# First expert layer: one product of 512 columns for both parts of x in every second block

## The chip, the cores and the metric
One core of a Trainium2 chip runs the kernel. The metric is the device time of one execution in microseconds, and it is given as the median of several runs. All data are float32; the large products run in the float32r form.

## The reference, cut to what matters
```python
x = x + gnn(layernorm(x), adj, Wq, Wk, Wv)      # 4096 rows of 256
xf = layernorm(x)
# the router picks 2 of E = 8 experts for each row
for e in range(8):
    h = relu(xf @ W1[e] + b1[e])                # W1[e]: 256 x 1024
    y = h @ W2[e] + b2[e]                       # W2[e]: 1024 x 256
    out = out + combine[:, e:e+1] * y
x = x + out
```
The kernel computes each expert for only those rows that chose it.

## The kernel before, in words
The first 440 us are attention and routing; the change leaves them alone. Then the experts run. The rows of an expert lie together in memory, and they are worked off in tiles of T = 256 rows (TS = 2 groups of 128). Here there are 37 tiles: 32 full ones and 5 half ones. Experts with an odd number of groups end with a half tile, for which TensorE streams 128 columns instead of 256, while the other engines still handle 256.

Each float32 operand is split in two float32r parts, a "hi" (the rounded value) and a "lo" (the rest). A product is then hi*hi + hi*lo + lo*hi. For a tile n the work is:

- **rows_turned** (L1372 to L1379): TensorE transposes the tile's rows into `psX`. ScalarE rounds them into `x_hi` (L1593, `part_of_x`), VectorE takes the rest into `x_lo` (L1076, `rest_of_x`). It is done for tile n+1 near the end of tile n, and the next tile's first product waits for `x_lo` (semaphore `xl_ready`, L1384).
- **first(hc)** (L1387 to L1394), eight times, for blocks of 128 hidden units: six products into one of four PSUM buffers `psH[:, hc % 4]`, of which columns 0 to 255 are used. It waits until the buffer's last block has been read (`hf_ready`, L1388).
- ScalarE (`tile_of`, L1603 to L1608) then applies bias and relu twice from the same PSUM buffer: to `h_f` in float32 (a piece of `z_all`, L1607) and to `h_hi` in float32r (L1608, signals `hf_ready`).
- VectorE (`tile`, L1111 to L1124) subtracts: `h_lo = h_f - h_hi` (L1122, signals `hl_ready`).
- **second(hc)** (L1396 to L1406): for each group of 128 rows a product of `h_hi` with both parts of the second weights side by side (512 columns, L1402) and one of `h_lo` with the large part (256 columns, L1404), into `psE`. It waits for `hl_ready` (L1397), and in block 0 for the previous tile's `psE` to be read, too (L1399).

TensorE's order is written out by hand with LAG = 3: first(0), first(1), first(2), first(3), second(0), first(4), second(1), ... first(7), second(4), rows_turned(n+1), second(5), second(6), second(7). All engines run their instructions in the order in which they are written.

VectorE has more to do in a tile. At the middle (hc == 4) it scales and adds the previous tile's result (`add_rows`, L1098, waits for rows gathered by GpSimd) and computes the gate (`gate_of`, L1084 to L1090). In an expert's first and second tile ("splitting tiles", 14 of 37) it also splits one piece of the next expert's weights in each odd block: `w_hi` (L1104) before the block's `h_lo`, `w_lo` (L1109) behind it. At the tile's end come `x_lo` (L1076), the copy of the row marks (L1079) and the sums of `psE` (L1133, L1136).

`wait_alone` (L344) is a wait as an instruction of its own, so that the value may come from a register.

Of the kernel before, what the change touches and what calls it, by code (L numbers as in the profile page):

```python
# [23 lines left out]
F32 = mybir.dt.float32  # L24
F32R = mybir.dt.float32r
# [8 lines left out]
ALU = mybir.AluOpType  # L34
ACT = mybir.ActivationFunctionType
AX = mybir.AxisListType

P = 128
# [7 lines left out]
CC = C // P  # L46
HC = H // P
# [12 lines left out]
T = 256  # L60
# [12 lines left out]
def attention_and_experts(nc, x, adj, Wq, Wk, Wv, Wr, W1, b1, W2, b2, out):  # L73
    ctx = ExitStack()

    def sb(name, shape, dt, stack=ctx):
        return stack.enter_context(nc.sbuf_tensor(name, shape, dt))
# [4 lines left out]
    def sem(name):  # L82
        return ctx.enter_context(nc.semaphore(name))

    with ctx:
# [149 lines left out]
        ffn = ExitStack()  # L235
# [3 lines left out]
        w1_lo = sb("w1_lo", [P, 2, CC, H], F32R, ffn)  # L239
        w2_parts = sb("w2_parts", [P, 2, HC, 2, C], F32R, ffn)  # L240
        x_in = sb("x_in", [P, TS, CX], F32, ffn)
        x_hi = sb("x_hi", [P, CC, T], F32R, ffn)
        x_lo = sb("x_lo", [P, CC, T], F32R, ffn)

        h_f = z_all[:].rearrange("p t c -> p (t c)")[:, 0:HC * T].rearrange("p (k t) -> p k t", t=T)
        b2_rows = z_all[:].rearrange("p t c -> p (t c)")[:, HC * T:HC * T + E * C].rearrange("p (e c) -> p e c", c=C)
# [85 lines left out]
        b2_loaded = sem("b2_loaded"); x_ps = sem("x_ps");  # L332
        w_raw = [sem("w1_raw_loaded"), sem("w2_raw_loaded")]; w_hi = sem("w_hi"); w_split = sem("w_split");
        xin_loaded = sem("xin_loaded"); xh_ready = sem("xh_ready"); xl_ready = sem("xl_ready")
        h_ps = sem("h_ps"); hf_ready = sem("hf_ready"); hl_ready = sem("hl_ready")
        e_ps = sem("e_ps"); yo_ready = sem("yo_ready"); yp_ready = sem("yp_ready")
        marks_ready = sem("marks_ready"); tok_taken = sem("tok_taken"); less_ready = sem("less_ready"); gate_step = sem("gate_step")
        acc_ready = sem("acc_ready"); acc_clear = sem("acc_clear"); y_ready = sem("y_ready"); y_scattered = sem("y_scattered"); y_free = sem("y_free"); tok_kept = sem("tok_kept")
# [5 lines left out]
        def wait_alone(eng, what, value):  # L344

            eng.wait_ge(what, value)
            if not isinstance(value, int):
                eng.sem_inc(passed[eng.engine], 1)
# [252 lines left out]
        def _(dve):  # L601
# [471 lines left out]

            def rest_of_x(n):
                dve.wait_ge(xh_ready, n + 1)
                dve.tensor_tensor(x_lo[:].rearrange("p k t -> p (k t)"), psX[:], x_hi[:].bitcast(F32).rearrange("p k t -> p (k t)"),  # L1076
                                  ALU.subtract).then_inc(xl_ready, 1)
                wait_alone(dve, tok_taken, n + 1)
                dve.tensor_copy(marks[:], x_in[:, :, TOK:TOK + 2].bitcast(U32)).then_inc(marks_ready, 1)  # L1079
# [21 lines left out]
            def next_weights_hi(e, c):  # L1101
                raw, hi, lo = weight_part(c, (e + 1) % 2)
                wait_alone(dve, w_raw[c // (SPLITS // 2)], e * 16 + 32)
                dve.tensor_copy(hi, raw).then_inc(w_hi, 1)  # L1104
# [6 lines left out]
            def tile(n, e, split=None, first=False, alone=None):  # L1111
                for hc in range(HC):
                    if hc == HC // 2:
                        if not first:
                            add_rows(n)
                        gate_of(n, e)
                    splitting = split is not None and hc % 2 == 1
                    c = (split or 0) * (SPLITS // 2) + hc // 2
                    if splitting:
                        next_weights_hi(e, c)  # L1120
                    dve.wait_ge(hf_ready, n * HC + hc + 1 + 4)
                    dve.tensor_tensor(h_lo[:, hc, :], h_f[:, hc, :], h_hi[:, hc, :].bitcast(F32), ALU.subtract).then_inc(hl_ready, 1)  # L1122
                    if splitting:
                        next_weights_lo(e, c)  # L1124
                if alone is not None:
                    with dve.If(alone):
                        for c in range(SPLITS // 2, SPLITS):
                            next_weights_hi(e, c)
                            next_weights_lo(e, c)
                rest_of_x(n + 1)  # L1130
                for q in range(TS):
                    dve.wait_ge(e_ps, n * TS + q + 1)
                    dve.tensor_tensor(y_part[:, q, :], psE[:, q, C:2 * C], row(b2_rows, e), ALU.add).then_inc(yp_ready, 1)  # L1133
                for q in range(TS):
                    wait_alone(dve, yp_ready, n * TS + q + 1)
                    dve.tensor_tensor(y_sum[:, q, :], psE[:, q, 0:C], y_part[:, q, :], ALU.add).then_inc(yo_ready, 1)  # L1136
# [23 lines left out]
        def _(pe):  # L1160
# [221 lines left out]
            def tile(n, b, parts):  # L1382

                wait_alone(pe, xl_ready, n + 1)  # L1384
                cols = slice(0, parts * P)

                def first(hc):  # L1387
                    wait_alone(pe, hf_ready, n * HC + hc + 1)  # L1388
                    m = slice(hc * P, (hc + 1) * P)
                    for k in range(CC):  # L1390
                        pe.matmul(psH[:, hc % 4, cols], w1_hi[:, b, k, m], x_hi[:, k, cols], start=(k == 0), stop=False)  # L1391
                        pe.matmul(psH[:, hc % 4, cols], w1_hi[:, b, k, m], x_lo[:, k, cols], start=False, stop=False)  # L1392
                        last = pe.matmul(psH[:, hc % 4, cols], w1_lo[:, b, k, m], x_hi[:, k, cols], start=False, stop=(k == CC - 1))  # L1393
                    last.then_inc(h_ps, 1)  # L1394

                def second(hc):  # L1396
                    wait_alone(pe, hl_ready, n * HC + hc + 1 + HC)  # L1397
                    if hc == 0:
                        wait_alone(pe, yo_ready, n * TS + TS)  # L1399
                    for q in range(parts):  # L1400
                        m = slice(q * P, (q + 1) * P)
                        pe.matmul(psE[:, q, :], h_hi[:, hc, m], w2_parts[:, b, hc].rearrange("p s c -> p (s c)"),  # L1402
                                  start=(hc == 0), stop=False)
                        last = pe.matmul(psE[:, q, 0:C], h_lo[:, hc, m], w2_parts[:, b, hc, 0, :], start=False, stop=(hc == HC - 1))  # L1404
                        if hc == HC - 1:
                            last.then_inc(e_ps, 1 if q + 1 < parts else TS - q)  # L1406
                for hc in range(HC + LAG):
                    if hc < HC:
                        first(hc)
                    if hc == HC:  # L1410
                        rows_turned(n + 1)
                    if hc >= LAG:
                        second(hc - LAG)
# [16 lines left out]
        def _(act):  # L1430
# [159 lines left out]

            def part_of_x(n):
                act.wait_ge(x_ps, n + 1 + 1)
                act.copy(x_hi[:].rearrange("p k t -> p (k t)"), psX[:]).then_inc(xh_ready, 1)  # L1593
                act.activation(less_exp[:], x_in[:, :, LESS], ACT.Exp).then_inc(less_ready, 1)
            part_of_x(0)

# [6 lines left out]
            def tile_of(n, e):  # L1603
                for hc in range(HC):
                    wait_alone(act, hl_ready, n * HC + hc + 1)
                    act.wait_ge(h_ps, n * HC + hc + 1)
                    act.activation(h_f[:, hc, :], psH[:, hc % 4, 0:T], ACT.Relu, bias=b1T[:, e * HC + hc:e * HC + hc + 1])  # L1607
                    act.activation(h_hi[:, hc, :], psH[:, hc % 4, 0:T], ACT.Relu, bias=b1T[:, e * HC + hc:e * HC + hc + 1]).then_inc(hf_ready, 1)  # L1608
                part_of_x(n + 1)
# [30 lines left out]
```

## Time and profile before

| | us |
|---|---|
| median of 3 runs (896.09 to 896.87) | 896.53 |
| the profiled execution, its own time | 893.15 |
| its span, first to last instruction | 891.4 |
| TensorE busy in it | 704.7 |
| VectorE busy | 574.5 |
| ScalarE busy | 455.6 |
| GpSimd busy | 428.0 |

The profile is one execution. A timeline row has the start of an instruction in us from the span's start, its duration in us, the engine (PE is TensorE's products, DVE VectorE, ACT ScalarE), the line, what it writes and reads, and, in brackets, how long the engine was idle before it and what ended that. Instructions of one engine overlap: the next one can start before the last one's end, so the distance between two starts (the pitch) is what an instruction costs in a dense stream, and its duration is what a waiting engine sees.

### The profile page before, as it was taken

How to read it: one execution, taken by the hardware profiler on the slowest of the kernel's cores; microseconds unless marked ns; L12 is line 12 of the kernel's file. 1: busy time of each engine (PE TensorE's matmuls, PEld its weight loads, DVE VectorE, ACT ScalarE, POOL GpSimd, SP SyncE). 2: the span in 40 equal slices, each digit the busy share in tenths (PEclk: the TensorE clock that was granted, in tenths of full speed). 3: DMA queues.
4: the chain of work that ended last, by engine and by line, in shares of the span. 5: the costliest groups of instructions: out<-in, count | busy, mean ns of one | idle time of the engine just before them, and what ended most of it. 6: DMA issues, size and time to landing. Idle time of an engine off the chain costs nothing.

```text
span 891.4 us, 22902 instructions
## 1 busy us (share of the span) xinstructions
PE 704.7 (79%) x6398; PEld 640.0 (72%) x6399; DVE 574.5 (64%) x2054; ACT 455.6 (51%) x1286; POOL 428.0 (48%) x482
## 2 busy tenths in 40 slices
PE   2559999999876724261299999999999999999994
PEld 1448888888763614260299888888988899898993
DVE  8745666666639697426185766767666685776554
ACT  2535665655561403242255666555556555656663
POOL 2177777777730187773224334333433344444433
PEclk8569999999997555565599999999999999999997
DMA  9875334551101222447623242233314242112121
GB/s 292 266 193 134 103 85 125 137 132 34 46 17 48 68 81 94 139 160 247 194 94 101 56 157 66 90 118 107 112 57 154 70 151 85 44 61 76 43 65 39
DMA packets 89586, 96.72 MB, mean 109 GB/s; under 512 B 10427, under 2 KB 78533, under 8 KB 89404
## 3 DMA queue, kind: packets, MB, share of 16 engines
q1 hardware_dynamic: 70860, 61.46, 23.5%
q0 software_dynamic: 18672, 34.66, 12.2%
q8 instruction: 20, 0.33, 0.2%
q14 instruction: 34, 0.28, 0.1%
HBM read 82.25 MB, written 30.33 MB: 126 GB/s over the span
## 4 chain that ended last, share of the span: by engine, by line
PE 32%; issue 7%; DMA 6%; DVE 3%; POOL 2%; SPq 1%; DVEq 1%; ACT 1%; POOLq 0%; ACTq 0%
PE psE L1402 10%; PE psH L1391 5%; PE psH L1393 5%; PE psH L1392 5%; PE psE L1404 5%; DMA acc<-out,tok_next 4%; POOL out L576 2%; PE psX L1378 2%; SPq L423 1%; DMA expert_in<-pad_row 1%; DVE y_out L1098 1%; DVE h_lo L1122 1%; DMA out<-y_out,tok_now 1%; SPq L424 0%; DVE w_parts L1109 0%
## 5 line engine op out<-in xcount | busy, mean ns | idle before, releaser
L1607 ACT ACTIVATE z_all<-psH,b1T 128x256 f32<-128x256 f32 x296 | 142.6, 482 | 160.3 <-PE psH L1393 159.7
L1402 PE MATMUL psE<-w_parts,h_hi 128*128 128x512 f32 x552 | 209.6, 406 | 3.4 <-DVE h_lo L1122 2.7
L493 POOL DMA_INDIRECT nbr<-xn_rows,idx x160 | 164.6, 1029 | 83.8 <-issue 81.6
L1122 DVE TENSOR_TENSOR h_lo<-z_all,h_hi 128x256 fp32r<-128x256 f32 x296 | 122.5, 424 | 81.3 <-ACT h_hi L1608 81.2
L1391 PE MATMUL psH<-x_hi,w_hi 128*128 128x256 f32 (+1 forms) x592 | 166.2, 281 | 10.7 <-issue 6.1
L1393 PE MATMUL psH<-x_hi,w_lo 128*128 128x256 f32 (+1 forms) x592 | 165.9, 280 | 0.0
L1392 PE MATMUL psH<-x_lo,w_hi 128*128 128x256 f32 (+1 forms) x592 | 165.6, 280 | 0.0
L1404 PE MATMUL psE<-w_parts,h_lo 128*128 128x256 f32 x552 | 154.9, 281 | 0.0
L1608 ACT ACTIVATE h_hi<-psH,b1T 128x256 fp32r<-128x256 f32 x296 | 142.1, 480 | 0.0
L576 POOL DMA_INDIRECT out<-y_out,tok_now x74 | 77.5, 1047 | 112.9 <-DVE y_out L1098 93.4
L1391 PEld LDWEIGHTS psH<-x_hi,w_hi 128*128 128x128 f32 x592 | 112.3, 190 | 21.8 <-issue 14.1
L1402 PEld LDWEIGHTS psE<-w_parts,h_hi 128*128 128x128 f32 x552 | 103.8, 188 | 20.9 <-issue 5.5
L1393 PEld LDWEIGHTS psH<-x_hi,w_lo 128*128 128x128 f32 x592 | 112.4, 190 | 0.0
L1392 PEld LDWEIGHTS psH<-x_lo,w_hi 128*128 128x128 f32 x592 | 112.4, 190 | 0.0
L1404 PEld LDWEIGHTS psE<-w_parts,h_lo 128*128 128x128 f32 x552 | 104.3, 189 | 0.0
L567 POOL DMA_INDIRECT acc<-out,tok_next x74 | 77.3, 1044 | 47.8 <-POOL tok_next L562 33.5
L690 DVE CUSTOM_DVE_ANT_0 prod<-q_sb,nbr 128x256 f32<-128x256 f32 x160 | 58.2, 423 | 60.2 <-DMA nbr<-xn_rows,idx 34.5
L521 POOL DMA_INDIRECT expert_in<-late,pos x64 | 67.6, 1056 | 37.5 <-issue 19.3
L1219 PEld LDWEIGHTS psY<-diag,nbr 128*128 128x128 f32 x640 | 80.0, 198 | 6.8 <-ACT diag L1471 5.1
L1219 PE MATMUL psY<-diag,nbr 128*128 128x128 f32 x640 | 80.3, 282 | 5.0 <-ACT diag L1471 5.0
L572 POOL COPY tok_now<-tok_next 128x2 uint32<-128x2 uint32 x37 | 8.2, 221 | 102.4 <-DMA acc<-out,tok_next 102.4
L1208 PE MATMUL psQ<-wqk,xT 128*128 128x256 f32 x128 | 38.1, 422 | 17.7 <-ACT xT L1482 17.7
(335 smaller groups left out, 1173.7 us busy)
## 6 DMA issues: line engine op xcount, KB each, us to landing
w_raw<-in_L_ffn_W SPq DMA_DIRECT2D x16, 1024.0 KB, 5.5
x_in<-expert_in SPq DMA_DIRECT2D x38, 260.0 KB, 3.1
adj_even<-in_adj SPq DMA_DIRECT2D x4, 2048.0 KB, 13.0
late<-in_adj SPq DMA_DIRECT2D x4, 2048.0 KB
x_all<-in_x SPq DMA_DIRECT2D x4, 1024.0 KB, 9.1
xn_rows<-z_all SPq DMA_DIRECT2D x4, 1024.0 KB
out<-x_all SPq DMA_DIRECT2D x4, 1024.0 KB, 4.6
expert_in<-pad_row SPq DMA_DIRECT2D x8, 390.0 KB, 8.4
```

The costliest lines, as they stand in the source:

```text
L493: pool.indirect_dma_start(nbr[:, u * K + k, :], None, xn_rows, bass.IndirectOffsetOnAxis(ap=idx[:, u, k:k + 1], axis=0), bounds_check=ROW0 ...
L567: pool.indirect_dma_start(acc[:, q, :], None, out, bass.IndirectOffsetOnAxis(ap=tok_next[:, q:q + 1], axis=0), bounds_check=N - 1, oob_is_ ...
L576: pool.indirect_dma_start(out, bass.IndirectOffsetOnAxis(ap=tok_now[:, q:q + 1], axis=0), y_out[:, q, :], None, bounds_check=N - 1, oob_is ...
L1122: dve.tensor_tensor(h_lo[:, hc, :], h_f[:, hc, :], h_hi[:, hc, :].bitcast(F32), ALU.subtract).then_inc(hl_ready, 1)
L1219: last = pe.matmul(psY[:, c * P:(c + 1) * P], nbr[:, u * K + k, c * P:(c + 1) * P], diag[:, u % 2 * K + k, :], start=(k == 0), stop=(k == ...
L1391: pe.matmul(psH[:, hc % 4, cols], w1_hi[:, b, k, m], x_hi[:, k, cols], start=(k == 0), stop=False)
L1392: pe.matmul(psH[:, hc % 4, cols], w1_hi[:, b, k, m], x_lo[:, k, cols], start=False, stop=False)
L1393: last = pe.matmul(psH[:, hc % 4, cols], w1_lo[:, b, k, m], x_hi[:, k, cols], start=False, stop=(k == CC - 1))
L1402: pe.matmul(psE[:, q, :], h_hi[:, hc, m], w2_parts[:, b, hc].rearrange("p s c -> p (s c)"), start=(hc == 0), stop=False)
L1404: last = pe.matmul(psE[:, q, 0:C], h_lo[:, hc, m], w2_parts[:, b, hc, 0, :], start=False, stop=(hc == HC - 1))
L1607: act.activation(h_f[:, hc, :], psH[:, hc % 4, 0:T], ACT.Relu, bias=b1T[:, e * HC + hc:e * HC + hc + 1])
L1608: act.activation(h_hi[:, hc, :], psH[:, hc % 4, 0:T], ACT.Relu, bias=b1T[:, e * HC + hc:e * HC + hc + 1]).then_inc(hf_ready, 1)
```

## The change
In odd blocks (hc = 1, 3, 5, 7) TensorE multiplies the large weights with `x_hi` and `x_lo` side by side: one product of 512 columns takes the place of two of 256 columns, for each k. Columns 0 to 255 of the PSUM buffer then hold the `x_hi` half (to which the `w1_lo` product is still added), columns 256 to 511 the `x_lo` half. ScalarE adds the bias to the second half and writes `h_f`; VectorE adds the first half to it; ScalarE applies relu to the sum and writes `h_hi`; VectorE applies relu to `h_f` and subtracts `h_hi` in one instruction. On VectorE the addition for block hc + 1 stands ahead of the `h_lo` of block hc. Even blocks are computed as before. In half tiles the merged product has 2 x 128 columns.

```diff
-        x_hi = sb("x_hi", [P, CC, T], F32R, ffn)
-        x_lo = sb("x_lo", [P, CC, T], F32R, ffn)
+        x_parts = sb("x_parts", [P, CC, 2, T], F32R, ffn)
+        x_hi, x_lo = x_parts[:, :, 0, :], x_parts[:, :, 1, :]
...
@@ VectorE, rest_of_x(n)
-                dve.tensor_tensor(x_lo[:].rearrange("p k t -> p (k t)"), psX[:], x_hi[:].bitcast(F32).rearrange("p k t -> p (k t)"),
+                dve.tensor_tensor(x_lo, psX[:].rearrange("p (k t) -> p k t", k=CC), x_hi.bitcast(F32),
                                   ALU.subtract).then_inc(xl_ready, 1)
...
@@ VectorE, tile(...)
                     if splitting:
                         next_weights_hi(e, c)
+                    if hc % 2 == 0:
+                        wait_alone(dve, ht_ready, n * (HC // 2) + hc // 2 + 1)
+                        dve.tensor_tensor(h_f[:, hc + 1, :], psH[:, (hc + 1) % 4, 0:T], h_f[:, hc + 1, :], ALU.add).then_inc(hs_ready, 1)
                     dve.wait_ge(hf_ready, n * HC + hc + 1 + 4)
-                    dve.tensor_tensor(h_lo[:, hc, :], h_f[:, hc, :], h_hi[:, hc, :].bitcast(F32), ALU.subtract).then_inc(hl_ready, 1)
+                    if hc % 2 == 0:
+                        dve.tensor_tensor(h_lo[:, hc, :], h_f[:, hc, :], h_hi[:, hc, :].bitcast(F32), ALU.subtract).then_inc(hl_ready, 1)
+                    else:
+                        dve.scalar_tensor_tensor(h_lo[:, hc, :], h_f[:, hc, :], 0.0, h_hi[:, hc, :].bitcast(F32), ALU.max, ALU.subtract).then_inc(hl_ready, 1)
                     if splitting:
                         next_weights_lo(e, c)
...
@@ TensorE, first(hc)
                     for k in range(CC):
-                        pe.matmul(psH[:, hc % 4, cols], w1_hi[:, b, k, m], x_hi[:, k, cols], start=(k == 0), stop=False)
-                        pe.matmul(psH[:, hc % 4, cols], w1_hi[:, b, k, m], x_lo[:, k, cols], start=False, stop=False)
+                        if hc % 2:
+                            pe.matmul(psH[:, hc % 4].rearrange("p (s t) -> p s t", s=2)[:, :, cols], w1_hi[:, b, k, m],
+                                      x_parts[:, k, :, cols], start=(k == 0), stop=False)
+                        else:
+                            pe.matmul(psH[:, hc % 4, cols], w1_hi[:, b, k, m], x_hi[:, k, cols], start=(k == 0), stop=False)
+                            pe.matmul(psH[:, hc % 4, cols], w1_hi[:, b, k, m], x_lo[:, k, cols], start=False, stop=False)
                         last = pe.matmul(psH[:, hc % 4, cols], w1_lo[:, b, k, m], x_hi[:, k, cols], start=False, stop=(k == CC - 1))
...
@@ ScalarE, tile_of(n, e)
                     wait_alone(act, hl_ready, n * HC + hc + 1)
+                    if hc % 2:
+                        wait_alone(act, hl_ready, n * HC + hc + 1)
+                        act.wait_ge(h_ps, n * HC + hc + 1)
+                        act.activation(h_f[:, hc, :], psH[:, hc % 4, T:2 * T], ACT.Identity, bias=b1T[:, e * HC + hc:e * HC + hc + 1]).then_inc(ht_ready, 1)
+                        act.wait_ge(hs_ready, n * (HC // 2) + hc // 2 + 1)
+                        act.activation(h_hi[:, hc, :], h_f[:, hc, :], ACT.Relu).then_inc(hf_ready, 1)
+                        continue
```
The cast into `x_hi` (L1593) gets the same reshaping as `x_lo`, and `hs_ready` and `ht_ready` are new semaphores.

## Rows read from the trace of the kernel before

**Rows 1.** The page: busy time of TensorE, and its granted clock over the span
```profile
PE 704.7 (79%) x6398; PEld 640.0 (72%) x6399; DVE 574.5 (64%) x2054; ACT 455.6 (51%) x1286; POOL 428.0 (48%) x482
...
PEclk8569999999997555565599999999999999999997
```

**Rows 2.** Waits of TensorE, 438 to 880 us: us in total, times, longest
```profile
PE psE L1402 <- DVE h_lo L1122: 2.7, 5, 1.0
```

**Rows 3.** Five tiles by window: busy PE, PEld, DVE, ACT, POOL; clock, DMA share, GB/s
```profile
619.65:631.69 12.04, 11.94 (x86) 10.99 (x85) 10.10 (x29) 7.09 (x18) 5.40 (x7) 1.00 0.44 153
607.90:619.65 11.75, 11.74 (x84) 11.05 (x85) 9.50 (x27) 7.08 (x18) 2.80 (x4) 1.00 0.14 46
857.96:869.64 11.68, 11.68 (x86) 10.96 (x85) 6.93 (x21) 7.08 (x18) 4.45 (x7) 1.00 0.23 67
489.52:499.62 10.10, 8.94 (x70) 8.17 (x69) 7.48 (x23) 7.08 (x18) 3.27 (x6) 1.00 0.24 70
869.64:878.59 8.95, 8.95 (x70) 8.15 (x68) 6.33 (x19) 7.09 (x18) 2.59 (x5) 1.00 0.22 67
```

**Rows 4.** Timeline: the start of a full tile without weight splitting, three engines
```profile
846.27 0.28 PE L1391 MATMUL psH<-x_hi,w_hi 128*128 128x256 f32 x1
...
847.54 0.47 ACT L1608 ACTIVATE h_hi<-psH,b1T 128x256 fp32r<-128x256 f32 x1
847.55 0.28 PE L1393 MATMUL psH<-x_hi,w_lo 128*128 128x256 f32 x1
...
847.90 0.48 ACT L1607 ACTIVATE z_all<-psH,b1T 128x256 f32<-128x256 f32 x1
...
848.04 0.43 DVE L1122 TENSOR_TENSOR h_lo<-z_all,h_hi 128x256 fp32r<-128x256 f32 x1 [0.49 <-ACT h_hi L1608]
...
849.07 0.40 PE L1402 MATMUL psE<-w_parts,h_hi 128*128 128x512 f32 x1
...
849.30 0.28 PE L1404 MATMUL psE<-w_parts,h_lo 128*128 128x256 f32 x1
```

**Rows 5.** Timeline: products of a half tile
```profile
489.80 0.27 PE L1391 MATMUL psH<-x_hi,w_hi 128*128 128x128 f32 x1
...
491.47 0.27 PE L1391 MATMUL psH<-x_hi,w_hi 128*128 128x128 f32 x1
```

**Rows 6.** Timeline: one tile's first h_lo and the product that waited for it
```profile
513.61 0.43 DVE L1122 TENSOR_TENSOR h_lo<-z_all,h_hi 128x256 fp32r<-128x256 f32 x1 [0.97 <-ACT h_hi L1608]
...
514.43 0.47 PE L1402 MATMUL psE<-w_parts,h_hi 128*128 128x512 f32 x1
```

**Rows 7.** Page and groups by line: nearest prices for the new instructions
```profile
L1136 DVE TENSOR_TENSOR y_sum<-psE,y_part 128x256 f32<-128x256 f32 x74 | 27.6, 415 | 0.2 <-DVE y_part L1133 0.2
L1444 ACT ACTIVATE z_all<-x_all,less_mean,rstd 128x256 f32<-128x256 f32 x24 | 12.1, 585 | 0.0
L1458 ACT COPY xt<-z_all 128x256 f32<-128x256 f32 x7 | 2.8, 403 | 0.0
```

**Rows 8.** Timeline: the end of the tile before the one in rows 4
```profile
843.21 0.47 ACT L1607 ACTIVATE z_all<-psH,b1T 128x256 f32<-128x256 f32 x1 [0.58 <-PE psH L1393]
...
844.35 0.59 ACT L1593 CAST x_hi<-psX 128x512 fp32r<-128x512 f32 x1 [0.30 <-PE psX L1378]
...
844.97 0.69 DVE L1076 TENSOR_TENSOR x_lo<-psX,x_hi 128x512 fp32r<-128x512 f32 x1 [0.43 <-ACT x_hi L1593]
```

**Rows 9.** Timeline of VectorE in the splitting tile 619.65 to 631.69
```profile
621.92 0.43 DVE L1122 TENSOR_TENSOR h_lo<-z_all,h_hi 128x256 fp32r<-128x256 f32 x1 [0.98 <-ACT h_hi L1608]
...
623.54 0.42 DVE L1122 TENSOR_TENSOR h_lo<-z_all,h_hi 128x256 fp32r<-128x256 f32 x1
...
625.72 0.88 DVE L1098 SCALAR_TENSOR_TENSOR y_out<-y_sum,gate,acc 128x256 f32<-128x256 f32 x2 [0.49 <-issue]
...
627.39 0.43 DVE L1122 TENSOR_TENSOR h_lo<-z_all,h_hi 128x256 fp32r<-128x256 f32 x1
...
630.62 0.68 DVE L1076 TENSOR_TENSOR x_lo<-psX,x_hi 128x512 fp32r<-128x512 f32 x1
```

More of the change, by code:

```diff
@@ L334, in attention_and_experts @@
         xin_loaded = sem("xin_loaded"); xh_ready = sem("xh_ready"); xl_ready = sem("xl_ready")
-        h_ps = sem("h_ps"); hf_ready = sem("hf_ready"); hl_ready = sem("hl_ready")
+        h_ps = sem("h_ps"); hf_ready = sem("hf_ready"); hs_ready = sem("hs_ready"); ht_ready = sem("ht_ready"); hl_ready = sem("hl_ready")
         e_ps = sem("e_ps"); yo_ready = sem("yo_ready"); yp_ready = sem("yp_ready")
@@ L1592, in part_of_x @@
                 act.wait_ge(x_ps, n + 1 + 1)
-                act.copy(x_hi[:].rearrange("p k t -> p (k t)"), psX[:]).then_inc(xh_ready, 1)
+                act.copy(x_hi, psX[:].rearrange("p (k t) -> p k t", k=CC)).then_inc(xh_ready, 1)
                 act.activation(less_exp[:], x_in[:, :, LESS], ACT.Exp).then_inc(less_ready, 1)
```

## The prediction
> **What bounds the kernel now.** I read the page first: TensorE is the busiest engine, and its clock is at its upper level, 2.4 GHz, through nearly all of the second half, where the change lies [rows 1]. Then the waits: over the whole expert stage TensorE waited 2.7 us for `h_lo`, in five places [rows 2]. Then the tiles one by one: in a full tile without weight splitting TensorE is busy for all of the 11.68 us [rows 3]. So the stage is a dense stream of TensorE, and everything ScalarE and VectorE do is hidden. The question is by how little. VectorE is busy 10.10 of 12.04 us in a splitting tile, and ScalarE 7.08 of 8.95 us in a half tile [rows 3]; both get more work here. The 37 tiles are 14 splitting, 18 full without splitting, 5 half.
>
> **TensorE: the merged product.** From 846.27 to 849.07 there are 24 products of 256 columns, 0.117 us each; the 512-column product has a pitch of 0.23 to the next [rows 4]. Two of 256 cost 0.234, so the merge buys between nothing and some 5 ns, the rounding of the row. I take 1 ns: 32 full tiles x 4 blocks x 2 = 256 pairs, 0.3 us. The Trainium skill (TensorE: Matmul & The Clock Gate, Back-to-back issue gap) gives about 131 ns per 512-column product as the sustained pace and would promise 256 x 0.10 = 26 us; the existing 512-column products show 0.23, and by that the page does not hold here.
>
> In a half tile 15 pitches take 1.67 us, 0.111 each for 128 columns [rows 5]: a merged product of 256 columns at 0.117 replaces two, 0.105 less. That is 8 per tile, 0.84 us, if TensorE still bounds there.
>
> **The longer chain at a tile's start.** Before: `h_hi` of block 0 starts at 847.54 and takes 0.47, `h_lo` starts at 848.04 and ends at 848.47. Where TensorE did wait for `h_lo`, its product came 514.43 - 514.04 = 0.39 us after the end (block 0 has two waits) [rows 6]. So second(0) could have started at 848.86; it started at 849.07, when the stream reached it [rows 4]. The slack is 0.21 us. Now VectorE must do the addition for block 1 ahead of that `h_lo`. ScalarE's first instruction of block 1 starts at 847.90, where L1607 did, and takes 0.48: 848.38. I add 0.15 for the signal and VectorE's separate wait (my choice: signals between engines show 0.03 to 0.04, as from 848.01, the end of `h_hi`, to 848.04 [rows 4], a separate wait some 0.1 more; bounds 0.04 and 0.25). The addition reads PSUM and SBUF like L1136, 0.415 us [rows 7]. A following `h_lo` starts some 0.34 later (four VectorE instructions in 1.62 us, one of them of 512 columns [rows 9]; its whole duration, 0.43, is the upper bound). So `h_lo` starts 848.53 + 0.34 = 848.87, ends 849.30, and second(0) starts 849.69: **0.61 us late**, in every full tile. Bounds 0.45 and 0.75.
>
> **The end of a tile.** ScalarE's last block starts at 843.21 [rows 8]. New: 0.48, 0.15, 0.42 for the addition, 0.04, then the relu, at 844.30. Its price isn't in the trace: a copy from SBUF to SBUF takes 0.403, an activation from SBUF with per-row bias and scale 0.585 [rows 7]. I take 0.40, as it reads neither bias nor scale, with a pitch of 0.31 (L1607 at 0.48 has about 0.36 to the next [rows 4], so overlap is 0.1). The Trainium skill (ScalarE: Activation LUTs) puts an ACTIVATE with immediate operands at 186 + 0.833 N ns, so 399 ns by an estimate from that page. The cast to `x_hi` then starts at 844.61 instead of 844.35, `x_lo` 0.26 later too. `x_lo` ended at 845.66, and with 0.39 the next tile could start at 846.05; it started at 846.27 [rows 4, 8]. Slack 0.22, so 0.05 us late. With the relu at 0.585 it is 0.2.
>
> Full tiles without splitting: 18 x (0.61 + 0.05) = 11.9 us. Inside such a tile the chain is covered: an odd block now takes 0.48 + 0.15 + 0.42 + 0.04 + 0.40 + 0.04 + 0.45, 2.0 us from PSUM to `h_lo`, while TensorE reaches its second() six segments of 0.70 later, 4.2 us.
>
> **Splitting tiles.** VectorE's pair of blocks (h_lo, w_hi, h_lo, w_lo) has a period of 623.54 - 621.92 = 1.62 us; the middle (y_out and gate) takes 627.39 - 625.72 = 1.67; `x_lo` starts at 630.62, and the next tile 0.39 after its end [rows 3, 9]. That is already a tight chain. The addition costs 0.34 a pair, the fused max and subtract 0.02 more: 1.98. VectorE starts 2.25 us into the tile (848.53 - 846.27) and doesn't pause: 2.25 + 4 x 1.98 + 1.67 + 0.68 + 0.39 = 12.9 us. Against 11.75 for an expert's first tile and 12.04 for its second that is +1.15 and +0.9 (its 0.49 us pause before y_out is filled): 7 x 2.05 = 14.4 us. I add 2.0 us (0.15 a tile) because second(4) and second(6), which need `h_lo` behind an addition, come within 0.2 us of VectorE's schedule. VectorE becomes the bound here.
>
> **Half tiles.** ScalarE's pair takes 0.37 + 0.36 for the even block, then 0.48 + 0.15 + 0.42 + 0.04 + 0.31: 2.13 us. TensorE needs 2 x 1.01 = 2.03 before and 1.82 after, so ScalarE bounds, standing still while VectorE adds. First activation at 0.87 (six products, result, signal), first relu at 2.69, fourth at 2.69 + 3 x 2.13 = 9.08. In the middle VectorE's 1.67 us stands between the `h_lo` of block 3 (ending its pitch at 5.6) and the addition of block 5, which so starts at 7.3 instead of 6.5: +0.8. The last relu starts at 9.85, `x_hi` 10.16 to 10.75, `x_lo` 10.79 to 11.48, next tile 11.87, against 10.10 [rows 3]: +1.75, four times. The kernel's last tile ends with second(7): relu until 10.25, `h_lo` 10.7, wait 0.2, products 0.5: 11.4 against 8.95: +2.45. Together 9.5 us. TensorE's 0.84 a tile is lost behind it.
>
> **Sum:** 11.9 + 14.4 + 2.0 + 9.5 - 0.3 = 37.5 us. The profiled execution took 893.15 (span 891.4 and 1.75 around it) and would take 930.6; the median lies 3.4 above the profiled time, so the median goes to 934.0. Three full tiles close an expert; their idle time for the change of expert may swallow the 0.05, no more. No DMA is added or moved; GpSimd is paced by `y_out` and slides with it.
>
> **Rivals.**
> - *A, the lag covers the chain* (faster). For it: three blocks of lead, and 2.0 us against 4.2 within a tile. Then only TensorE's own saving counts: 0.3 + 5 x 0.84 = 4.5, 892.0 us. It decides at the start of a tile: addition and its handover would have to cost under 0.21 us, and L1136 alone speaks against it. If moreover a merged product went at the pace of one of 256 columns, 256 x 0.117 = 30 us would go, 866; the 0.23 speaks against that. By the page's 131 ns it would be about 870. Chance 4% for all of it, 1% of it for the pace.
> - *B, only tiles' starts are hurt* (VectorE and ScalarE overlap better than in my chains; the 0.49 us pauses show room): 37 x 0.66 = 24.4, 921. 20%.
> - *C, the forecast*: 934. 55%.
> - *D, the handshake binds in every pair*: relu 0.585, a handover 0.25, VectorE slowed beside other traffic. 18 x 0.95, 7 x (1.9 + 1.4), 4 x 2.6 + 3.2: 54 us, 950. 18%.
> - *E, nothing measurable*: half-tile gain and stalls cancel; needs most of B to vanish. 3%.
>
> **How the numbers follow.** What can be told from no change is about 0.2%, 1.8 us. Faster is A, same E, slower B, C and D. The range: the low ends of my costs (0.45 x 18, splitting 12.7 us, half +1.0) give 22 to 24 us, B at a lower handover 18; the high ends are D's, up to 57. So 914 to 954.
>
> **What the profile after would show.** The 512-column product of the first layer with a pitch of 0.23. In a plain tile: waits of L1402 on `h_lo` of about 0.6 us once a tile, and a length of 12.35. In splitting tiles: 12.9 to 13.1, VectorE without idle time between the first addition and `x_lo`. In half tiles: ScalarE waiting for the addition 0.6 us in every pair, 11.9 us in all. TensorE's clock stays at 2.4 GHz, as its pauses stay short. I would be wrong if second(0) started on time, if the merged product's pitch were under 0.2, or if the splitting tiles kept to 12.

## The result and the profile after

The changed kernel takes 945.28 us (median of 3 runs, 944.59 to 947.32) against 896.53: a ratio of 1.055, 95% interval 1.052 to 1.058. It is 48.8 us slower. The forecast was 934.0, slower, with a range of 914 to 954. The sign held, and so did the mechanism in splitting and half tiles; in plain tiles (full, without splitting) a longer chain counts than the one that was forecast, and the size was some 11 us short. The profiled execution took 944.59 us, its span is 942.8.

The page of the changed kernel, busy time and granted clock, to be read beside [rows 1]:

```profile
span 942.8 us, 22921 instructions
PE 723.8 (77%) x6102; PEld 630.0 (67%) x6103; DVE 626.9 (66%) x2202; ACT 449.6 (48%) x1286; POOL 433.0 (46%) x482
...
PEclk8569999999976555555999999999999999999997
```

TensorE issues 296 products less. VectorE is busy 52 us more; the 148 additions of 0.425 us add up to 62.9, and where instructions overlap the busy time counts once. ScalarE is busy less than before: its relu of the odd blocks, which reads SBUF and adds no bias, takes 0.418 us, the one from PSUM with bias 0.467. No engine is short of time by these sums; the loss shows as waits. What TensorE waited for in the expert stage (440 to 932 us), and what ScalarE waited for:

```profile
PE psE L1412 <- DVE h_lo L1126: 27.2, 43, 1.2
...
PE psH L1401 <- issue: 11.6, 13, 1.8
PE psH L1401 <- DVE x_parts L1076: 8.0, 14, 1.7
```
```profile
ACT h_hi L1621 <- DVE z_all L1123: 116.6, 148, 1.9
```

TensorE's wait for `h_lo` was 2.7 us before [rows 2] and is 27.2 us, mostly once a tile. All three waits come to 46.8 us, for 13.4 before. TensorE's busy time grew, too, by 19.1 us to 723.8, with fewer products. Part of that is waiting too: the profile counts a product's whole duration (0.28 us) as busy, while the next one could start after 0.117, so a pause looks shorter than the delay that it makes (below, 0.43 us idle for 0.59 late). Part is a lower clock in three tiles (last section). ScalarE now stands 116.6 us for VectorE's additions, 0.60 us in a usual odd block and 0.79 in the mean of the 148.

Six tiles by window (as in [rows 3]: length, busy PE, PEld, DVE, ACT, POOL, clock, DMA share, GB/s): plain, an expert's second splitting tile, its first one, half, the tile behind that half tile, and the last half tile.

```profile
894.12:906.68 12.56, 12.12 (x76) 10.58 (x77) 8.41 (x25) 6.95 (x18) 4.51 (x6) 1.00 0.21 63
642.22:655.61 13.39, 12.41 (x77) 10.57 (x77) 11.50 (x34) 6.96 (x18) 6.36 (x7) 1.00 0.38 139
629.00:642.22 13.22, 12.30 (x76) 10.57 (x77) 10.48 (x30) 6.85 (x18) 2.64 (x4) 1.00 0.11 38
496.19:509.18 12.99, 8.91 (x60) 7.52 (x61) 8.89 (x27) 6.74 (x18) 5.07 (x7) 1.00 0.21 64
509.18:523.41 14.23, 13.75 (x77) 12.02 (x77) 10.69 (x31) 6.97 (x18) 3.19 (x5) 0.88 0.10 25
919.49:931.27 11.78, 8.87 (x60) 7.47 (x60) 7.70 (x23) 6.73 (x18) 4.21 (x6) 1.00 0.22 67
```

Every kind of tile got longer. Taken over the trace, from a tile's first product to the next tile's:

| kind of tile | before, mean us | after, mean us | together, us | forecast, us |
|---|---|---|---|---|
| 18 full without splitting | 12.12 | 13.02 | +16.2 | +11.9 |
| 14 splitting | 12.11 | 13.52 | +19.8 | +16.4 |
| 5 half | 10.05 | 12.88 | +14.2 | +9.5 |

Together that is +50.2 us. The expert stage also began 2.5 us later than in the profile of before (443.3 against 440.7 us) and its tail was 1.3 us shorter, which gives the 51.4 us between the two spans. The medians differ by less, 48.8, as the profiled execution of before was 3.4 us faster than its median and that of the changed kernel 0.7. The late start is no effect of the change: `merged_only`, below, starts its stage at 444.3 us and has a span of 892.1, and `before_lag4`, which has nothing of the change, starts it at 443.4.

The start of the plain tile whose counterpart is in [rows 4], in the changed kernel:

```profile
895.83 0.47 ACT L1619 ACTIVATE z_all<-psH,b1T 128x256 f32<-128x256 f32 x1
...
896.45 0.42 DVE L1123 TENSOR_TENSOR z_all<-psH,z_all 128x256 f32<-128x256 f32 x1 [1.21 <-ACT z_all L1619]
...
896.79 0.42 DVE L1126 TENSOR_TENSOR h_lo<-z_all,h_hi 128x256 fp32r<-128x256 f32 x1
...
896.91 0.42 ACT L1621 ACTIVATE h_hi<-z_all 128x256 fp32r<-128x256 f32 x1 [0.60 <-DVE z_all L1123]
...
897.60 0.47 PE L1412 MATMUL psE<-w_parts,h_hi 128*128 128x512 f32 x1 [0.43 <-DVE h_lo L1126]
```

The tile began at 894.12. ScalarE's bias instruction ends at 896.30, the addition starts 0.15 later, `h_lo` another 0.34 later and ends at 897.21, and the product comes 0.39 after that. 897.60 is 3.48 us into the tile, where the kernel before was at 2.80: 0.59 late by the pitch of the product ahead of it and 0.09 from a slower start. ScalarE's second wait for `hl_ready` in odd blocks, which stands in the diff, shows no price: L1619 starts 0.35 us behind L1625 (895.48), as L1607 started 0.36 behind L1608 before [rows 4].

### The profile page after: what moved, and what is told of

Same layout as the page of the kernel before. It is cut to its first block, busy times and chain, and to the rows that moved or that the text cites. A ratio compares the mean times of both kernels' runs of the same rounds, so it can differ in the third digit from the quotient of the medians.

```text
span 942.8 us, 22921 instructions
## 1 busy us (share of the span) xinstructions
PE 723.8 (77%) x6102; PEld 630.0 (67%) x6103; DVE 626.9 (66%) x2202; ACT 449.6 (48%) x1286; POOL 433.0 (46%) x482
## 4 chain that ended last, share of the span: by engine, by line
PE 24%; DVE 12%; issue 11%; ACT 5%; DMA 1%; SPq 1%; DVEq 1%; POOL 1%; ACTq 0%; POOLq 0%
PE psE L1412 8%; PE psE L1414 4%; PE psH L1403 3%; DVE h_lo L1126 3%; PE psH L1401 3%; PE psH L1398 3%; ACT z_all L1619 2%; PE psH L1402 2%; ACT h_hi L1625 2%; DVE x_parts L1076 1%; DVE z_all L1123 1%; DVE y_out L1098 1%; DVE w_lo L1109 1%; PE psX L1384 1%; DVE w_parts L1109 1%
## 5 line engine op out<-in xcount | busy, mean ns | idle before, releaser
L1412 PE MATMUL psE<-w_parts,h_hi 128*128 128x512 f32 x552 | 213.7, 411 | 27.6 <-DVE h_lo L1126 27.2
L1403 PE MATMUL psH<-x_parts,w_lo 128*128 128x256 f32 (+1 forms) x592 | 166.2, 281 | 0.0
L1123 DVE TENSOR_TENSOR z_all<-psH,z_all 128x256 f32<-128x256 f32 x148 | 62.9, 425 | 103.7 <-ACT z_all L1619 102.2
L1621 ACT ACTIVATE h_hi<-z_all 128x256 fp32r<-128x256 f32 x148 | 61.8, 418 | 116.6 <-DVE z_all L1123 116.6
L1403 PEld LDWEIGHTS psH<-x_parts,w_lo 128*128 128x128 f32 x592 | 115.0, 194 | 0.0
L1624 ACT ACTIVATE z_all<-psH,b1T 128x256 f32<-128x256 f32 x148 | 68.5, 463 | 93.6 <-PE psH L1403 93.4
L1398 PE MATMUL psH<-x_parts,w_hi 128*128 128x512 f32 (+1 forms) x296 | 108.7, 392 | 0.0
L1401 PE MATMUL psH<-x_parts,w_hi 128*128 128x256 f32 (+1 forms) x296 | 86.6, 293 | 19.8 <-issue 11.6
L1402 PE MATMUL psH<-x_parts,w_hi 128*128 128x256 f32 (+1 forms) x296 | 84.2, 285 | 0.0
L1401 PEld LDWEIGHTS psH<-x_parts,w_hi 128*128 128x128 f32 x296 | 57.3, 194 | 35.3 <-issue 30.4
L1619 ACT ACTIVATE z_all<-psH,b1T 128x256 f32<-128x256 f32 x148 | 70.3, 475 | 20.7 <-PE psH L1403 19.5
L1128 DVE SCALAR_TENSOR_TENSOR h_lo<-z_all,h_hi 128x256 fp32r<-128x256 f32 x148 | 62.9, 425 | 13.7 <-ACT h_hi L1621 11.6
```

The lines of the kernel that those rows point to most:

```text
L1123: dve.tensor_tensor(h_f[:, hc + 1, :], psH[:, (hc + 1) % 4, 0:T], h_f[:, hc + 1, :], ALU.add).then_inc(hs_ready, 1)
L1398: pe.matmul(psH[:, hc % 4].rearrange("p (s t) -> p s t", s=2)[:, :, cols], w1_hi[:, b, k, m], x_parts[:, k, :, cols], start=(k == 0), stop ...
L1619: act.activation(h_f[:, hc, :], psH[:, hc % 4, T:2 * T], ACT.Identity, bias=b1T[:, e * HC + hc:e * HC + hc + 1]).then_inc(ht_ready, 1)
```

## The experiments

Twelve kernels; each is compared with runs of the kernel before on the same chip. Tile lengths are from one profile each. The plain tile used is the last but two, which starts at 894.12 in the changed kernel and at 846.27 in the kernel before, or, in only_block_1 and only_block_5, the next one. It is the shortest of its neighbours in the changed kernel (12.74, 12.56, 12.81 us; before, all three took 11.69), so means over all tiles are given where they matter.

**1. merged_only.** Only TensorE's part of the change; the odd blocks' `x_lo` half is left out of the result.

```diff
-                    if hc % 2 == 0:
-                        wait_alone(dve, ht_ready, n * (HC // 2) + hc // 2 + 1)
-                        dve.tensor_tensor(h_f[:, hc + 1, :], psH[:, (hc + 1) % 4, 0:T], h_f[:, hc + 1, :], ALU.add).then_inc(hs_ready, 1)
...
-                    if hc % 2:
-                        wait_alone(act, hl_ready, n * HC + hc + 1)
...
```


> TensorE keeps the merged product in the odd blocks; ScalarE and VectorE are as in the kernel before and read only columns 0 to 255, so the x_lo half of the odd blocks is left out of the result. Theory H (the loss is the handshake between ScalarE and VectorE, the product costs what the two cost): 892 to 896 us; the merged product's pitch to the next is 0.23 us, plain full tiles 11.69 us, half tiles up to 0.8 us shorter. Rival P (the wide product or its operand layout is dear on TensorE): well over 905 us, with plain tiles over 12 us.

Measured: 895.49 us, 0.998 of before (0.997 to 0.999). The window of the plain tile and of a half tile:

```profile
847.06:858.72 11.66, 11.66 (x79) 10.60 (x77) 7.05 (x21) 7.08 (x18) 4.46 (x7) 1.00 0.23 67
813.96:823.67 9.71, 8.32 (x63) 7.42 (x61) 7.08 (x22) 6.95 (x18) 2.89 (x6) 1.00 0.25 72
```
The time and both kinds of tile lie where theory H had them. 11.66 for 11.68 in the plain tile: eight merged products save 0.02 us or so. That is all the change can bring there. In half tiles TensorE is busy 0.6 us less (8.32 for 8.95), but they are only 0.3 us shorter in the mean (9.73 for 10.05). The whole gain of the idea, with the addition for nothing, is 1.7 us, and by the interval between 0.5 and 3.

**2. split_products.** The changed kernel with the merge undone on TensorE alone.

```diff
-                            pe.matmul(psH[:, hc % 4].rearrange("p (s t) -> p s t", s=2)[:, :, cols], w1_hi[:, b, k, m],
-                                      x_parts[:, k, :, cols], start=(k == 0), stop=False)
+                            pe.matmul(psH[:, hc % 4, cols], w1_hi[:, b, k, m], x_hi[:, k, cols], start=(k == 0), stop=False)
+                            pe.matmul(psH[:, hc % 4, T:T + parts * P], w1_hi[:, b, k, m], x_lo[:, k, cols], start=False, stop=False)
```


> The changed kernel, but TensorE makes two products of 256 columns again in odd blocks, one into columns 0 to 255, one into 256 to 511; ScalarE and VectorE work as in the changed kernel. H: 944 to 947 us, as the changed kernel (945.3): TensorE's saving is 1 ns a pair in full tiles and hidden in half tiles. P: back towards 900 us.

Measured: 945.63 us, the changed kernel's time, as expected. With merged_only it splits the change in two: the loss is on ScalarE's and VectorE's side, and within 1 or 2 us the merge neither makes nor mends any of it.

**3. add_behind.** The three lines of VectorE's addition stand behind `h_lo` of block hc.

> The changed kernel, with VectorE's addition for block hc + 1 moved behind the h_lo of block hc instead of ahead of it. H: the wait of 0.6 us for h_lo at the start of each plain tile goes (18 tiles, 11 us), the splitting tiles gain about 0.3 us each as VectorE starts earlier (4 us), half tiles about 0.3 us: 926 to 933 us. Rival Q (it is only VectorE's added time, wherever it stands): 942 us or more.

Measured: 955.34 us (1.058 to 1.071 of before), 10 us slower than the changed kernel. The expectation failed on its sign. The product second(0) of a plain tile was on time, as expected, but another one was late, at the other end of the tile (timeline of the plain tile, a product of second(7); then the tile's window):

```profile
915.08 0.47 PE L1412 MATMUL psE<-w_parts,h_hi 128*128 128x512 f32 x1 [0.46 <-DVE h_lo L1125]
```
```profile
903.46:916.16 12.70, 12.10 (x77) 10.59 (x77) 8.57 (x25) 6.73 (x18) 4.71 (x7) 1.00 0.20 62
```
So the 0.6 us at the tile's start is not a loss that stands alone. ScalarE stood 2.04 us in the middle of the tile (1.10 in the changed kernel), because y_out, the gate and now also `h_lo` of block 4 stood ahead of the addition for block 5:

```profile
911.92 0.42 ACT L1621 ACTIVATE h_hi<-z_all 128x256 fp32r<-128x256 f32 x1 [2.04 <-DVE z_all L1128]
```
In the splitting tile that was read VectorE got a pause of 0.15 us in three of four pairs, since the relu was later than the `h_lo` that wants it. My new theory: each tile has one chain through ScalarE and VectorE from end to end, and TensorE's waits only show where the slack runs out first.

**4. all_full.** TensorE treats half tiles as full ones (`tile(before + full, b, TS)`).

> The changed kernel, with TensorE treating the five half tiles as full ones (twice the columns, same result). H: in half tiles ScalarE and VectorE set the pace (12.9 us), so TensorE's extra 2.7 us a tile cost nothing, the half tiles stay at 12.5 to 13 us, and the stretches of 3.4 us at 1.2 GHz behind three of them go, 0.9 us each: 940 to 944 us. If TensorE or its waits set the pace in half tiles: up to 5 x 2.7 = 13 us more, 958 us.

Measured: 944.15 us, where 940 to 944 was expected. The half tile and the tile behind it:

```profile
788.67:802.24 13.57, 12.13 (x77) 10.59 (x77) 9.17 (x27) 6.95 (x18) 5.60 (x7) 1.00 0.20 60
802.24:815.62 13.38, 12.37 (x77) 10.60 (x77) 10.63 (x31) 6.95 (x18) 2.98 (x6) 1.00 0.09 22
```
TensorE was busy 3.2 us longer in the half tile, and the tile only 0.2 us (13.35 in the changed kernel; the five in the mean 13.26 for 12.88, slightly over what was expected; of the 1.9 us that this makes for all five, 0.8 lie in the last one). ScalarE and VectorE set its pace. The tile behind it fell from 14.16 to 13.38 us, with the granted clock at 1.00 in place of 0.88.

**5. dve_load.** The kernel before plus VectorE's added time alone.

```diff
+                    if hc % 2 == 0:
+                        dve.tensor_tensor(spare[:, hc // 2, :], b2_rows[:, 0, :], b2_rows[:, 1, :], ALU.add)
```


> The kernel before, with one more VectorE addition of 256 columns (constants, into unused memory, nobody waits for it) ahead of the h_lo of each even block: VectorE's added time without the handshake. If VectorE's added time by itself makes the loss in splitting tiles: 14 tiles by 0.4 to 0.9 us, 902 to 910 us, plain tiles still 11.69 us. If the loss is that ScalarE and VectorE wait for each other (H): under 902 us, and the rest of the 49 us belongs to the waiting.

The added instruction takes 0.42 us, like the addition. Measured: 902.65 us, 1.007 of before (1.005 to 1.009), at the lower edge of what was expected if the load alone made the loss of the splitting tiles. The plain tile and a second splitting tile:

```profile
858.30:869.95 11.65, 11.65 (x86) 10.95 (x85) 8.15 (x25) 7.08 (x18) 4.88 (x7) 1.00 0.21 67
627.36:640.30 12.94, 12.37 (x85) 11.02 (x85) 11.47 (x34) 7.08 (x18) 6.13 (x7) 1.00 0.39 143
```
VectorE's load alone costs 6 us of the 49. Its profile, of an execution 2.8 us slower than the median, has them almost wholly in splitting tiles: 7.8 us over the 14, of the 19.8 that the change adds to them, with 0.9 in the half tiles and 0.4 in the 18 plain ones. So in splitting tiles the load alone explains a good third. If load and waiting simply add up, which was not tested, some 42 us are left to the waiting for each other.

**6. only_block_1 and 7. only_block_5.** The change in one odd block a tile (`if hc == 1`, `if hc == 5` in place of `if hc % 2`, and one count a tile for the two semaphores).

> The changed kernel with the merged product and the addition in block 1 alone; blocks 3, 5 and 7 as in the kernel before. H: a quarter of the additions, but all of the wait at a tile's start: plain tiles 12.3 us, together 912 to 920 us. If each merged block costs the same: 896.5 + 49 / 4 = 909 us.

> The same with block 5 alone, whose chain lies in the middle of a tile, behind VectorE's y_out and gate. H: no wait at the start; plain tiles 11.69 to 11.75 us, splitting tiles 0.1 to 0.4 us longer, half tiles up to 1 us: 899 to 906 us. If each merged block costs the same: 909 us.

Measured: 914.97 us (1.019 to 1.023) and 905.63 us (1.009 to 1.013). The plain tile with block 1, then with block 5:

```profile
878.91:891.29 12.38, 11.95 (x84) 10.96 (x83) 7.27 (x22) 7.14 (x18) 4.58 (x7) 1.00 0.22 63
```
```profile
868.25:879.93 11.68, 11.68 (x85) 10.89 (x84) 7.45 (x22) 7.02 (x18) 4.47 (x7) 1.00 0.22 68
```
Both times lie in the range of theory H, and not at the 909 of equal shares, though the second is only 3.4 us from it. The price of a merged block depends on where it stands: 18.6 us for block 1, 9 us for block 5, of which nothing in the plain tile shown (1.4 us over all 18) and half in the half tiles (11.04 us in the mean, for 10.05). Blocks 3 and 7 were not tried alone.

**8. behind_gate_late.** As add_behind, with the gate two blocks later.

```diff
-                    if hc == HC // 2:
-                        if not first:
-                            add_rows(n)
-                        gate_of(n, e)
+                    if hc == HC // 2 and not first:
+                        add_rows(n)
+                    if hc == HC // 2 + 2:
+                        gate_of(n, e)
```


> The addition behind h_lo as in add_behind (955.3), and VectorE's gate (0.86 us) moved from in front of block 4 to in front of block 6, so that only y_out stands ahead of the addition for block 5. Add_behind had its wait of 0.6 us moved from the start of a plain tile to its end, with ScalarE standing 2.0 us for the addition of block 5. If that middle stretch makes it: plain tiles fall to 11.9 to 12.2 us and half tiles by 0.7 us, 938 to 944 us. If the middle doesn't matter: 952 to 956 us.

Measured: 942.80 us, 12.5 less than add_behind; plain tile 12.13 us for 12.70, half tiles 12.67 for 13.30 in the mean. All of it is as expected, within 0.1 us. Taking 0.86 us out of the way of one addition, without taking any work off VectorE, bought that: it follows from the chain theory, and not from VectorE's load. The splitting tiles stayed as they were in add_behind (13.8 us in the mean).

**9. lag4 and 10. lag4_behind_gate_late.** `LAG = 4`.

> The changed kernel with TensorE's second products four blocks behind the first ones instead of three (LAG = 4), so that the first h_lo of a tile is due 0.7 us later. If the wait of 0.6 us at the tile's start is the whole loss of a plain tile: plain tiles 11.8 to 11.9 us, together about 931 us. If the chain of ScalarE and VectorE through the whole tile (first activation, four pairs of 2.12 us, one with y_out and gate in it, x_hi, x_lo) is itself 12.4 us long: plain tiles 12.3 to 12.5 us, the wait moves from h_lo to x_lo, together 940 to 944 us.

> LAG = 4 together with behind_gate_late (942.8), whose chain through a plain tile is shorter (gate in a pause, 12.13 us a tile). If the chain sets the length: 12.0 to 12.1 us for plain tiles still and 940 to 943 us. If TensorE's waits had set it: 11.7 us, 933 us.

Measured: 947.35 and 945.07 us, 3.4 and 2.1 us over what the chain theory gave and 2 us over the same kernels with LAG = 3, but far from 931 and 933. The plain tile of lag4, and the product in it that was late, again one of the last (second(6)):

```profile
894.91:907.32 12.41, 12.12 (x76) 10.58 (x77) 8.46 (x26) 6.73 (x18) 4.66 (x7) 1.00 0.21 64
...
905.63 0.48 PE L1412 MATMUL psE<-w_parts,h_hi 128*128 128x512 f32 x1 [0.24 <-DVE h_lo L1126]
```
12.41 us is the chain's length that the expectation gave, for 12.56 with the wait at the start; in the other kernel 12.18. A whole block of slack bought TensorE 0.15 us, in this tile and in the mean of the 18. The totals came out higher in part by no fault of the tiles: in both profiles the expert stage starts 1.9 us later than with LAG = 3 (445.1 and 445.2 for 443.3 us), while lag4's 37 tiles together are 0.9 us shorter than the changed kernel's. Among all profiles the start of the stage lies between 440.7 and 445.2 us, and whether LAG moves it is open. Among the tiles the first splitting ones got 0.2 us longer, and the stretches with a low clock behind half tiles were longer.

**11. vector_rounds.** VectorE takes ScalarE's relu over, so that ScalarE does not wait (with semaphores of their own for even and odd blocks).

```diff
-                        act.wait_ge(hs_ready, n * (HC // 2) + hc // 2 + 1)
-                        act.activation(h_hi[:, hc, :], h_f[:, hc, :], ACT.Relu).then_inc(hf_ready, 1)
...
+                        dve.wait_ge(hs_ready, n * (HC // 2) + hc // 2 + 1)
+                        dve.tensor_scalar(h_hi[:, hc + 1, :], h_f[:, hc + 1, :], 0.0, None, ALU.max).then_inc(ho_ready, 1)
```


> The changed kernel, but VectorE itself makes h_hi of odd blocks (max with 0, rounded) behind h_lo of the even block; ScalarE's odd block is the one instruction with the bias, and it no longer waits for VectorE. H: half tiles lose ScalarE's pauses and fall from 12.9 to 10.2 to 10.9 us; plain tiles to 12.1 to 12.4 us; splitting tiles get 4 x 0.34 us more VectorE and rise from 13.5 to 14.2 to 14.8 us; together 938 to 948 us. If VectorE's load alone were the matter, all three kinds would get longer, over 955 us.

Measured: 945.60 us. Plain, half and first splitting tile:

```profile
894.70:907.33 12.63, 12.13 (x77) 10.59 (x77) 9.02 (x30) 5.73 (x14) 4.48 (x6) 1.00 0.21 63
857.77:869.41 11.64, 8.87 (x60) 7.46 (x61) 9.44 (x31) 5.61 (x14) 3.68 (x6) 1.00 0.19 57
630.04:643.72 13.68, 12.68 (x76) 10.57 (x77) 11.06 (x34) 5.73 (x14) 2.88 (x4) 1.00 0.10 35
```
The total fell where expected, the parts did not: half tiles 11.60 us in the mean (12.88 in the changed kernel, 10.2 to 10.9 expected), splitting tiles 13.9 (13.5; 14.2 to 14.8 expected), the plain tile 12.63, no shorter at all (12.1 to 12.4 expected). Half tiles gain 6.4 us in all from a ScalarE that does not wait; what VectorE takes on costs 5.4 in the splitting tiles.

**12. before_lag4.** The kernel before, not the changed one, with one more block of lag.

```diff
-            LAG = 3
+            LAG = 4
...
+                if not isinstance(n, int) or n > 0:
+                    act.wait_ge(gate_step, n * 4 - 2)
                 act.activation(less_exp[:], x_in[:, :, LESS], ACT.Exp).then_inc(less_ready, 1)
```


> The kernel before with LAG = 4 (and one more wait on ScalarE ahead of its exp, which the reordering needs). The waits for h_lo of 0.25 to 1.2 us that the kernel before has at the start or in the middle of second and third tiles, some 6 us in all, should go: 889 to 894 us, plain tiles 11.69 us. If those tiles are held by x_lo or by the rows that GpSimd gathers anyway: 895 to 898 us.

Measured: 889.59 us, 0.991 of before (0.989 to 0.993). TensorE's waits in its expert stage:

```profile
PE psH L1391 <- DVE x_lo L1076: 2.7, 3, 1.7
PE psE L1402 <- DVE h_lo L1122: 0.3, 1, 0.3
```
This version beats both kernels, as expected. TensorE had waited 2.7 us for `h_lo` [rows 2], and 0.3 remains; its waits for `x_lo` fell from 4.6 to 2.7. Most of the gain is in the full tiles that follow the splitting ones (plain tiles 4.7 us in all). Plain tiles at the end of the stage stay at 11.69 us, TensorE's own time. Lag helps the kernel in which ScalarE and VectorE are shorter than TensorE and merely late at times; it does not help the one in which their chain is the longer one.

## Why the prediction was right or wrong

- **The merged product**: right. The 512-column product has a pitch of 0.233 us to the next (median of 256), two of 256 columns 0.234. The pace of about 131 ns for 512 columns that the Trainium skill gives (TensorE: Matmul & The Clock Gate, Back-to-back issue gap) does not fit this case; merged_only would have been near 870 us by an estimate from it and is at 895.5.
- **Half tile saving of 0.84 us, hidden**: right. Half tiles take 12.88 us in the mean in the changed kernel and in split_products; without the cover merged_only showed 0.3 us of the saving.
- **The first `h_lo` of a tile, 0.61 us late**: right as a time (0.59), the steps too: 0.15, 0.34, 0.39 came out to 0.01 us. (The prediction counts one instruction of 512 columns among the four behind the 0.34; there are two, `w_hi` and `w_lo`. The addition and `h_lo` are 0.34 apart all the same.) But I took it for a cost that stands alone. add_behind removed it and lag4 covered it, and a plain tile stayed at 12.70 and 12.41 us. What bounds a plain tile is the chain of ScalarE and VectorE as a whole. (In the changed kernel's plain tile ScalarE waited for TensorE ahead of block 5, too, which cost nothing, as VectorE was still at the gate, and ahead of block 7, which cost some 0.2 us.) That is the step that failed: the clause that "inside such a tile the chain is covered" looked at one block's 2.0 us against 4.2 us of lead, and not at how the pairs queue: 2.12 us each, and one with y_out and gate ahead of its addition. The relu of block 5 in the plain tile, which stood behind them:

```profile
902.27 0.42 ACT L1621 ACTIVATE h_hi<-z_all 128x256 fp32r<-128x256 f32 x1 [1.10 <-DVE z_all L1123]
```
- **The end of a tile, 0.05 us late**: mis-sized, 0.21 (from second(0) to the next tile 9.08 us for 8.89, with 0.02 saved by the merge). The relu took 0.418 us. TensorE's next product came 0.48 us after `x_lo`, not 0.39. I read this so, without a run that isolates it: TensorE's own instructions for the loop now began only behind the wait for the last `h_lo`. What speaks for it is that the gap behind the last product of second(7) grows with what stands there: 0.25 to 0.30 us ahead of a plain tile, 0.54 in the five places where a half tile follows, and it was 0.12 in both before. The end of the plain tile:

```profile
904.91 0.57 ACT L1603 CAST x_parts<-psX 128x512 fp32r<-128x512 f32 x1
...
905.03 0.42 DVE L1128 SCALAR_TENSOR_TENSOR h_lo<-z_all,h_hi 128x256 fp32r<-128x256 f32 x1 [0.15 <-ACT h_hi L1621]
...
905.51 0.69 DVE L1076 TENSOR_TENSOR x_parts<-psX,x_parts 128x512 fp32r<-128x512 f32 x1
...
906.68 0.36 PE L1401 MATMUL psH<-x_parts,w_hi 128*128 128x256 f32 x1
```
- **Splitting tiles**: right in mechanism (VectorE runs from the first addition to `x_lo` with hardly a pause), 12.9 to 13.1 forecast, 13.2 to 13.4 usual. The pair took 2.12 us instead of my 1.98: I had counted VectorE's instructions as a dense stream, but the next addition waits for ScalarE's bias instruction, which stands behind the last addition's relu. 2.12 is ScalarE's period, the one I had worked out for half tiles only. Two successive additions in the first splitting tile:

```profile
631.33 0.42 DVE L1123 TENSOR_TENSOR z_all<-psH,z_all 128x256 f32<-128x256 f32 x1 [2.61 <-ACT z_all L1619]
...
633.45 0.43 DVE L1123 TENSOR_TENSOR z_all<-psH,z_all 128x256 f32<-128x256 f32 x1
```
- **Half tiles**: the pair's 2.13 us was right (2.12), and ScalarE waits 0.60 us in every pair, as forecast, but for the middle one (1.74). Two terms failed. With y_out and gate, the last relu starts 10.18 us into the tile, not 9.85. And at a change of expert the first product comes 1.19 us after the end of `x_lo`, not 0.39: 509.18 against 507.99. In the program TensorE's loads and branches for the new expert stand behind second(7), and the first product starts 1.48 us after the last one of second(7), where it was 1.44 before. Four times 0.8 us is two thirds of the miss there. It could have been read from the trace of before: behind `x_lo` that gap was already 0.9 us (twice) and 1.3 us (twice). ScalarE in the half tile that starts at 496.19, the relus of blocks 5 and 7:

```profile
504.26 0.42 ACT L1621 ACTIVATE h_hi<-z_all 128x256 fp32r<-128x256 f32 x1 [1.74 <-DVE z_all L1123]
...
506.37 0.42 ACT L1621 ACTIVATE h_hi<-z_all 128x256 fp32r<-128x256 f32 x1 [0.60 <-DVE z_all L1123]
```
- **"TensorE's clock stays at 2.4 GHz"**: wrong. See below, 2.8 us, of which 1.8 in splitting tiles and 1.0 in a plain one.
- **The sum**: 37.5 forecast, 48.8 measured. The miss by kind of tile is 4.3 (plain), 3.4 (splitting) and 4.7 us (half), 12.4 in the profiles and 11.3 between the medians. All three err in the same direction.
- **Rivals**: A fell with the result; merged_only shows besides that without the handshake it would have been worth 1.7 us and not 4.5, and that the wide product has no faster pace. B (only the tiles' starts) would have been 921. D had the right place, the handshake binding in every pair, and was priced at 950; the truth lies between C and D, nearer to D. But D's reason was wrong: no single cost was at its upper bound. That the time lies in the range is luck in part, since the upper half of the range was made of these prices.

## What to carry to other kernels

A stage that is a dense stream of one engine can hide a fixed amount of work on the others, and the hidden engines' own chain, from the first hand-over of a tile to the last, has to be added up as a chain: a hand-over from ScalarE to VectorE and back inside one block puts each engine's wait into the other's period. Before saving columns or weight loads on TensorE, read the pitch of the wide product that is already in the trace; here it said that there was nothing to save. Where, as in before_lag4, the covering engines are short enough but late at times, one more block of lag is worth more (0.9%), as long as the buffers have room.

## What the runs showed of the hardware that was not expected

TensorE's clock fell to its lower level behind three of the four half tiles of the changed kernel that another tile follows. In a half tile TensorE was busy 8.91 of 12.99 us, in short bursts with waits of 0.7 to 1.2 us between. Before, it was busy 8.94 of 10.10 us in the same tile, and the clock stayed up [rows 3]. The first 5 us of the next tile, then two of its products:

```profile
509.18:514.18 5.00, 5.00 (x23) 4.54 (x24) 1.93 (x6) 2.53 (x7) 0.52 (x2) 0.66 0.23 58
```
```profile
509.72 0.42 PE L1401 MATMUL psH<-x_parts,w_hi 128*128 128x256 f32 x1
509.94 0.41 PE L1402 MATMUL psH<-x_parts,w_hi 128*128 128x256 f32 x1
```
A product of 256 columns had a pitch of 0.21 us, at 1.2 GHz, for 0.117 at 2.4 GHz. The lower clock cost 0.8 to 1.0 us in each of the three tiles, 2.8 us in all by the comparison with all_full, where TensorE is kept busy and the clock stays up. Why it did not happen behind the fourth, whose pauses were of the same length, is open. So a wait can cost more than its own length.
